# Cross-attention on one core: loads ordered by first use, attention values in one run, last projections in halves, new orders

## What is computed

```python
qh = _split_heads(q @ Wq.T + bq)          # q = x, 4 x 2048 x 512
kh = _split_heads(k @ Wk.T + bk)          # k = v = ctx, 4 x 77 x 512
vh = _split_heads(v @ Wv.T + bv)
scores = jnp.einsum('bhqd,bhkd->bhqk', qh, kh) / scale
scores = jnp.where(mask == 0, jnp.asarray(-1000000000.0, scores.dtype), scores)
m = jnp.max(scores, axis=-1, keepdims=True)
e = jnp.exp(scores - m) * mask.astype(scores.dtype)
probs = e / (jnp.sum(e, axis=-1, keepdims=True) + 1e-09)
attn = jnp.einsum('bhqk,bhkd->bhqd', probs, vh)
out = attn @ Wo.T + bo
x = out + residual
return (x - mu) / jnp.sqrt(var + 1e-05) * ln_g + ln_b
```

## Time and profile before

| | us |
|---|---|
| median of three runs | 617.84 (616.43 to 618.41) |
| the profiled execution | 615.88 |
| its span, first to last instruction | 614.1 |
| TensorE busy | 564.5 (92%) |
| VectorE busy | 525.6 (86%) |
| ScalarE busy | 504.6 (82%) |
| GpSimd busy | 437.5 (71%) |
| TensorE's mean granted clock | 0.985 |

### The profile page before, as it was taken

How to read it: one execution, slowest core, us unless ns; L and a number is a source line. 1 busy time by engine, 2 the same in 40 slices (tenths; PEclk the granted TensorE clock), 3 DMA queues, 4 the chain that set the end, 5 groups by cost and what they waited for, 6 DMA issues and landing times.

```text
span 614.1 us, 15264 instructions
## 1 busy us (share of the span) xinstructions
PE 564.5 (92%) x5460; PEld 456.9 (74%) x5460; DVE 525.6 (86%) x801; ACT 504.6 (82%) x2288; POOL 437.5 (71%) x399
## 2 busy tenths in 40 slices
PE   2699398999999999999999999999999999999795
PEld 2588376777878788777877788777878788776574
DVE  4577558789998979898998989898998899899877
ACT  4449669899898989998898989998898999889521
POOL 2704443867588795789778886689678967786787
PEclk9989789999999999999999999999999999999899
DMA  8922730120045310640324412340424312202132
GB/s 310 318 88 57 225 88 1 52 99 3 11 140 188 138 53 10 216 147 3 94 93 155 155 64 75 122 148 3 126 76 141 153 51 104 105 2 99 76 138 102
DMA packets 36198, 64.91 MB, mean 106 GB/s; under 512 B 12443, under 2 KB 14491, under 8 KB 34075
## 3 DMA queue, kind: packets, MB, share of 16 engines
q1 hardware_dynamic: 35979, 63.94, 30.6%
q10 hardware_dynamic: 144, 0.00, 0.0%
HBM read 44.15 MB, written 19.46 MB: 104 GB/s over the span
## 4 chain that ended last, share of the span: by engine, by line
PE 84%; DVE 6%; SPq 5%; DMA 3%; issue 2%; POOL 0%; ACT 0%; DVEq 0%
PE qo_bank L420 54%; PE s_bank L420 17%; PE av_bank L508 11%; DVE E L803 2%; DMA Kd<-TP 2%; PE av_bank L420 1%; DMA Vp<-V_scratch 1%; DVE TP L832 1%; SPq L251 1%; SPq L330 1%; SPq L256 1%; DVE qo_bank L849 1%; DVE bn L855 1%; SPq L304 0%; DVE AT_lo L841 0%
## 5 line engine op out<-in xcount | busy, mean ns | idle before, releaser
L625 ACT ACTIVATE E<-E,neg_max 128x77 f32<-128x77 f32 x1024 | 352.2, 352 | 19.7 <-DVE neg_max L811 19.6
L625 ACT ACTIVATION_READ_ACCUMULATOR E<-E,neg_max 128x1 f32 x1024 | 196.8, 192 | 0.0
L1125 POOL TENSOR_TENSOR E<-E,inv_sum 128x1232 f32<-128x1232 f32 x64 | 145.7, 2279 | 66.6 <-DVE inv_sum L818 66.6
L803 DVE TENSOR_TENSOR E<-s_bank,mask_bias 128x616 f32<-128x616 f32 x128 | 101.3, 791 | 40.7 <-PE s_bank L420 38.9
L420 PE MATMUL s_bank<-Kd,QT_hi 128*128 128x308 f32 x512 | 111.7, 305 | 0.0
L832 DVE STREAM_TRANSPOSE TP<-E 128x1280 f32<-128x1280 f32 x64 | 96.1, 1502 | 4.1 <-PE av_bank L508 3.6
L811 DVE TENSOR_REDUCE neg_max<-E 128x8 f32<-128x624 f32 x128 | 98.5, 781 | 0.4
L420 PE MATMUL s_bank<-Kd,QT_lo 128*128 128x308 f32 x256 | 81.3, 317 | 15.5 <-DVE E L803 11.7
L420 PEld LDWEIGHTS s_bank<-Kd,QT_hi 128*128 128x128 f32 x512 | 84.4, 188 | 4.2
L1143 POOL TENSOR_TENSOR Y<-Y,b_row 128x512 f32<-128x512 f32 x62 | 79.2, 1297 | 4.5 <-ACT Y L642 4.2
L1105 POOL TENSOR_TENSOR xT_lo<-xT_raw,xT_hi 128x1024 fp32r<-128x1024 f32 x30 | 71.7, 2410 | 14.0 <-ACT xT_hi L602 14.0
(11 more groups left out here) (60 smaller groups left out, 790.9 us busy)
## 6 DMA issues: line engine op xcount, KB each, us to landing
Y<-in_x SPq DMA_DIRECT2D x16, 1024.0 KB, 6.1
out_y<-Y SPq DMA_DIRECT2D x64, 256.0 KB, 2.0
xT_raw<-in_xT SPq DMA_DIRECT2D x15, 1024.0 KB, 4.9
Vp<-V_scratch SPq DMA_DIRECT2D x32, 96.0 KB, 2.4
K_scratch<-TP SPq DMA_DIRECT2D x1, 1232.0 KB, 6.8
Y<-in_WqT SPq DMA_DIRECT2D x4, 256.0 KB, 8.4
xT_raw<-in_xT SPq DMA_DIRECT2D x2, 512.0 KB, 6.9
TP<-in_WvT SPq DMA_DIRECT2D x4, 256.0 KB, 7.9
```

The source lines that it names most:

```text
L625: last = cp(e, e, ACT.Exp, bias=neg_max[:, t, h:h + 1], accum_out=rowsum[:, t, h:h + 1])
L803: tt(E[:, t, :, 0:SK].rearrange("p (g j) k -> p g j k", g=2), s_bank[:, :, 0:GK].rearrange("p g (j k) -> p g j k", j=HG), mask_bias[:, row ...
L1125: nc.gpsimd.tensor_tensor(out=e, in0=e, in1=inv.unsqueeze(2).broadcast_to((P, 2 * HH, SK)), op=ALU.mult).then_inc(probs_ready, 1)
```

## The change

The transfers of the opening are put in another order: x of block 0 goes ahead of `WqT`, in two pieces with a semaphore each (`x_first`), x of block 1 ahead of the mask, and `load_K(0)` is issued ahead of all later weights (`later_loads`), of which `WqT`'s second half now leads. Block 1's high part is made by GpSimd (`XT_hi_1`), its low part by VectorE (`XT_lo_first(1, i)`), and GpSimd also casts the second half of `WqT` (`split_hi_q`). On TensorE the two halves of `AV` stand next to each other in every block, where 13 of 16 blocks had a score unit between them. The output projection of block 14 is cut into two parts of six matmuls (`OUT_first` with channels 0 and 1, then `OUT` with channels 2 and 3), its last two row groups in `s_bank`. `S` itself, the tiles and all arithmetic stay. The orders of all five engines are new: `OUT` runs one turn later against the scores than it did, loads of x are issued in the turns before their use, and the written-out turns at both ends differ. Of the diff the parts that the text speaks of are shown; the new orders of ScalarE, VectorE and the rest of GpSimd's are left out, as are TensorE's turns 4, 14 and 15, of which 4 and 14 keep three neighbouring scores as the even pattern has them.

```diff
+        x_first = [sem(f"x_first{i}") for i in range(2)]
+        x1_hi = sem("x1_hi")
+        wq_hi_1 = sem("wq_hi_1")
...
+        QO_TURN = ((("Q", 1, 1), ("OUT", 4, 0), ("Q", 1, 2), ("OUT", 4, 1), ("Q", 1, 3),
+                    ("OUT", 4, 2), ("OUT", 4, 3), ("Q", 0, 0)),
+                   (("Q", 1, 1), ("OUT", 4, 0), ("Q", 1, 2), ("Q", 1, 3), ("OUT", 4, 1),
+                    ("OUT", 4, 2), ("OUT", 4, 3), ("Q", 0, 0)))
...
+        def split_out(o):
+            return o == NB - 2
+
+        def out_bank(o, k):
+            return s_bank[:, k - 2, :] if split_out(o) and k >= 2 else qo("OUT", o, k)[:, :]
...
-                for i in range(2 if b == 0 else 1):
-                    cs = slice(2 * i, 2 * i + 2) if b == 0 else slice(0, C)
-                    sp.dma_start(xT_raw[:, b % 2, cs, :], xT[b, :, cs, :]).then_inc(x_loaded[b % 2], 16)
+                sp.dma_start(xT_raw[:, b % 2, :, :], xT[b]).then_inc(x_loaded[b % 2], 16)
+
+            def load_xT_first():
+                for i in range(2):
+                    cs = slice(2 * i, 2 * i + 2)
+                    sp.dma_start(xT_raw[:, 0, cs, :], xT[0, :, cs, :]).then_inc(x_first[i], 16)
...
             load_half("k", WkT, 0)
+            load_xT_first()
             load_half("q", WqT, 0)
-            load_xT(0)
+            load_xT(1)
             sp.dma_start(mask_i, mask).then_inc(mask_loaded, 16)
-            load_xT(1)
-            load_half("k", WkT, 1)
-            load_half("q", WqT, 1)
-            for c in range(C):
-                load_w("v", WvT, c)
-            load_row(bv_loaded, bv_row[:, :], bv)
-            zero_V()
-            for c in range(C):
-                load_w("o", WoT, c)
-            load_row(bo_loaded, bo_row[:, :], bo)
-            load_row(rows_loaded, g_row[:, :], ln_g)
-            load_row(rows_loaded, b_row[:, :], ln_b)
+
+            def later_loads():
+                load_half("q", WqT, 1)
+                load_half("k", WkT, 1)
+                for c in range(C):
+                    load_w("v", WvT, c)
+                load_row(bv_loaded, bv_row[:, :], bv)
+                zero_V()
+                for c in range(C):
+                    load_w("o", WoT, c)
+                load_row(bo_loaded, bo_row[:, :], bo)
+                load_row(rows_loaded, g_row[:, :], ln_g)
+                load_row(rows_loaded, b_row[:, :], ln_b)
+
             for s in range(-3, NB + 6):
+                if s == -3:
+                    next_xT(0), next_xT(1), load_K(0), later_loads(), save_K()
+                elif s == -2:
+                    next_xT(2)
...
-                    next_xT(s - 2), next_xT(s - 1), next_K(s - 2), next_K(s - 1), store(s - 6, 0)
-                    store(s - 6, 1), store(s - 6, 2), store(s - 6, 3), store(s - 5, 0), load_rows(s - 4)
-                    store(s - 5, 1), store(s - 5, 2), store(s - 5, 3)
+                    next_K(s - 1), store(s - 5, 0), store(s - 5, 1), store(s - 5, 2), store(s - 5, 3)
+                    load_rows(s - 3), next_xT(s), next_xT(s + 1), next_V(s - 1)
                 else:
-                    load_rows(s - 5), store(s - 6, 0), store(s - 6, 1), store(s - 6, 2), store(s - 6, 3)
+                    store(s - 5, 0), store(s - 5, 1), store(s - 5, 2), store(s - 5, 3), next_V(s - 1)
+                    next_K(s - 1), load_rows(s - 3)
...
+            def OUT_part(o, k, cs, first, last):
+                pair, j = o // 2, 4 * (o % 2) + k
+                i, cols = j // 2, slice(j % 2 * P, j % 2 * P + P)
+                pe.wait_ge(at_lo, 4 * (2 * pair + cs[-1] // 2) + i + 1)
+                products = [(a[:, AT_PLACE[2 * pair + c // 2, i], c % 2, cols], w[:, c, :])
+                            for a, w in ((AT_hi, WoT_lo), (AT_lo, WoT_hi), (AT_hi, WoT_hi)) for c in cs]
+                for n, (a, b) in enumerate(products):
+                    done = mm(out_bank(o, k), a, b, start=first and n == 0, stop=last and n == len(products) - 1)
+                return done
+
+            def OUT_first(o, k):
+                if not has(o):
+                    return
+                if k < 2:
+                    qo_free("OUT", o, k)
+                else:
+                    pe.wait_ge(biased, T2 * NB)
+                OUT_part(o, k, (0, 1), True, False)
+
             def OUT(o, k):
                 if not has(o):
                     return
+                if split_out(o):
+                    OUT_part(o, k, (2, 3), False, True).then_inc(out_ps, 1)
+                    return
                 qo_free("OUT", o, k)
-                pair, j = o // 2, 4 * (o % 2) + k
-                i, cols = j // 2, slice(j % 2 * P, j % 2 * P + P)
-                pe.wait_ge(at_lo, 4 * (2 * pair + 1) + i + 1)
                 if o == 0 and k == 0:
                     pe.wait_ge(w_lo["o"], C)
-                accumulate(qo("OUT", o, k)[:, :],
-                           [(a[:, AT_PLACE[2 * pair + c // 2, i], c % 2, cols], w[:, c, :])
-                            for a, w in ((AT_hi, WoT_lo), (AT_lo, WoT_hi), (AT_hi, WoT_hi)) for c in range(C)]) \
-                    .then_inc(out_ps, 1)
+                OUT_part(o, k, range(C), True, True).then_inc(out_ps, 1)
 
             for s in range(-3, NB + 6):
                 if s == -3:
-                    K(0), K(1)
+                    K(0), K(1), Q(0, 0), Q(0, 1), Q(0, 2), S(0, 0), K(2), K(3), S(0, 1), Q(0, 3), S(0, 2)
+                elif s == -2:
+                    V(0), S(0, 3)
                 elif s == -1:
-                    Q(0, 0), Q(0, 1)
+                    V(1), V(2), S(0, 4), Q(1, 0), S(0, 5)
                 elif s == 0:
-                    K(2), K(3), S(0, 0)
+                    Q(1, 1)
                 elif s == 1:
-                    Q(0, 2), S(0, 1), Q(0, 3), S(0, 2), V(0), S(0, 3), V(1), S(0, 4), V(2), S(0, 5), Q(1, 0)
-                    S(0, 6), Q(1, 1), S(0, 7), Q(1, 2), S(1, 0), Q(1, 3), S(1, 1), S(1, 2), AV(0, 0)
-                    AV(0, 1), S(1, 3), S(1, 4)
+                    S(0, 6), S(0, 7)
                 elif s == 2:
-                    Q(2, 0), S(1, 5), Q(2, 1), S(1, 6), Q(2, 2), S(1, 7), S(2, 0), Q(2, 3), S(2, 1), S(2, 2)
-                    S(2, 3), Q(3, 0), S(2, 4), AV(1, 0), S(2, 5)
+                    Q(1, 2), Q(1, 3), S(1, 0), S(1, 1), S(1, 2), S(1, 3), Q(2, 0), S(1, 4), S(1, 5)
+                    AV(0, 0), AV(0, 1), S(1, 6)
                 elif s == 3:
-                    AV(1, 1), S(2, 6), Q(3, 1), OUT(0, 0), Q(3, 2), Q(3, 3), OUT(0, 1), S(2, 7), S(3, 0)
-                    OUT(0, 2), S(3, 1), OUT(0, 3), S(3, 2), Q(4, 0), S(3, 3), AV(2, 0)
-                elif s == 13:
-                    AV(11, 1), Q(13, 1), S(12, 5), OUT(10, 0), S(12, 6), Q(13, 2), OUT(10, 1), S(12, 7)
-                    Q(13, 3), S(13, 0), OUT(10, 2), S(13, 1), OUT(10, 3), S(13, 2), Q(14, 0), S(13, 3)
-                    AV(12, 0)
+                    Q(2, 1), S(1, 7), S(2, 0), Q(2, 2), Q(2, 3), S(2, 1), S(2, 2), S(2, 3), Q(3, 0)
+                    AV(1, 0), AV(1, 1), S(2, 4)
...
                 elif s == 16:
-                    S(15, 2), S(15, 3), AV(14, 0), S(15, 4), AV(14, 1), S(15, 5), OUT(13, 0)
+                    S(14, 2), Q(15, 0), S(14, 3), AV(13, 0), AV(13, 1), S(14, 4), Q(15, 1), S(14, 5)
+                    OUT(12, 0), S(14, 6), Q(15, 2), S(14, 7), OUT(12, 1), S(15, 0), Q(15, 3), S(15, 1)
+                    OUT(12, 2), OUT(12, 3)
                 elif s == 17:
-                    S(15, 6), S(15, 7), OUT(13, 1), OUT(13, 2), OUT(13, 3)
+                    S(15, 2), S(15, 3), S(15, 4)
                 elif s == 18:
-                    AV(15, 0), AV(15, 1)
+                    AV(14, 0), AV(14, 1), S(15, 5)
+                elif s == 19:
+                    pass
+                elif s == 20:
+                    OUT(13, 0), S(15, 6), S(15, 7)
                 elif s == 21:
-                    OUT(14, 0), OUT(14, 1), OUT(14, 2), OUT(14, 3), OUT(15, 0), OUT(15, 1), OUT(15, 2)
-                    OUT(15, 3)
+                    OUT(13, 1), OUT(13, 2), OUT(13, 3), OUT_first(14, 0), AV(15, 0), AV(15, 1)
+                    OUT_first(14, 1), OUT(14, 0), OUT(14, 1), OUT_first(14, 2), OUT_first(14, 3), OUT(14, 2)
+                    OUT(14, 3), OUT(15, 0), OUT(15, 1), OUT(15, 2), OUT(15, 3)
                 elif s % 2 == 0:
-                    S(s - 1, 4), AV(s - 2, 1), S(s - 1, 5), Q(s, 1), OUT(s - 3, 0), S(s - 1, 6), Q(s, 2)
-                    S(s - 1, 7), OUT(s - 3, 1), S(s, 0), Q(s, 3), OUT(s - 3, 2), S(s, 1), OUT(s - 3, 3)
-                    S(s, 2), Q(s + 1, 0), S(s, 3), AV(s - 1, 0), S(s, 4)
+                    AV(s - 3, 0), AV(s - 3, 1), S(s - 2, 4), Q(s - 1, 1), S(s - 2, 5), OUT(s - 4, 0)
+                    S(s - 2, 6), Q(s - 1, 2), OUT(s - 4, 1), S(s - 2, 7), Q(s - 1, 3), S(s - 1, 0)
+                    OUT(s - 4, 2), OUT(s - 4, 3), S(s - 1, 1), S(s - 1, 2), S(s - 1, 3), Q(s, 0)
+                    S(s - 1, 4), AV(s - 2, 0), AV(s - 2, 1), S(s - 1, 5)
                 else:
```

(37 more changed lines are left out.)

686 lines of the change are left out of this document (323 added, 363 removed).

## The result

The changed kernel took 623.22 us (621.5 to 626.03, four executions) against 617.13 for the kernel before: a ratio of 1.0106, interval 1.0054 to 1.0157. The forecast was 614.8, a gain of 3. The profiled execution took 621.89, with a span of 620.1; the sum had 611.1.

| stage | before | forecast | changed |
|---|---|---|---|
| start to end of `AV(2)` | 149.67 | 139.6 | 144.93 |
| to end of `AV(12)` | 342.35 | 347.7 | 351.83 |
| to the end | 122.1 | 123.8 | 123.3 |

A forecast was written before the change was run, and what follows sets the result against it. It took TensorE's own list to bound the middle, with waits counting at both ends. Opening -10.0, middle +5.3 and ending +1.7 gave -3.0, carried from the median 617.84 to 614.8 us, range 605 to 623.

The forecast's parts named there:

- Step (f): Opening: `Vp` load issued near 64, landing near 71; `turn(0, 3)` late next; `AV(0)` runs from 73.3 to 77.5.
- step (g): Opening: after `AV(1)`, TensorE's own units bring `AV(2)` to its end at 139.6 against 149.67, the -10.0.
- Steps (a) to (d): Opening: first matmul at 8.2 instead of 11.28, no wait at `Q(0, 0)`, 0.7 allowed at `Q(0, 2)`, `S(0, 0)` at 22.5.
- (c): Opening: `Q(0, 2)` needs x of block 1, cast and subtracted near 19, when TensorE arrives; 0.7 allowed.
- Step (e): Opening: `K(2)` waits about 3 for `WkT`'s late second half, and what follows is slow; 4.5 counted.
- (i): Middle: an `S` directly follows an `S` in 10 places instead of 4; six more at 1.18 are +7.1.
- (h): Middle: `AV` in one run saves 0.34 a block, 3.4 over the ten blocks from `AV(3)` to `AV(12)`.
- (j): Middle: whole `AV` runs may break off, costing 0 to 0.8 a block; two of ten taken, 1.6.
- (k): Middle: VectorE keeps up, 32.9 a block against 34.6, three margins under 0.5; 0 taken, 1 us per block as bad end.
- Rival (2): Every `AV` in one run breaks off: 13 more runs at 0.8, 10.4 instead of 1.6; 623.6, slower; chance 0.12.
- Rival (4): Opening gives half: `WkT` split meets GpSimd's casts, exponentials start 4 us later; -6 instead of -10, 618.8; chance 0.12.
- Rivals (1) and (3): (1): waits cheaper, no `AV` breaks, ending gains, 607.5, chance 0.22. (3): VectorE bounds the middle, 620.8, chance 0.12.

The follow-up runs named there:

- the second profile: The changed kernel timed and profiled again with no edit, beside the kernel before: 625.94 us, ratio 1.0140.
- keys_early: The changed kernel with `load_K(1)` issued ahead of `next_xT(2)` on SyncE: 618.68 us, ratio 1.0038 to the kernel before.
- merged_halves: Changed kernel's opening with early keys' load, then the kernel before's order, `AV` halves apart, `S(s - 1, 7)` ahead of `Q(s, 3)`, `center` moved earlier: 604.09 us, ratio 0.9788.
- join_center_first: As before_join, with `center(s - 4, 3)` ahead of `bias(s - 1, 4)` on VectorE in the even turns 4 to 14: 619.60 us, ratio 1.0044.
- one_pair: The changed kernel with the three scores in a row taken apart in even turns, five direct S-S successions instead of ten: 617.21 us, ratio 1.0011.
- far_pairs: As one_pair, plus a second S-S succession in the odd turns: ten successions, none right behind another: 625.80 us, ratio 1.0158.
- before_join: The kernel before with the two halves of `AV` joined for blocks 2 to 12: 635.32 us, ratio 1.0295.
- before_nopair: As before_join, with `S(s - 1, 7)` ahead of `Q(s, 3)` in odd turns 5 to 11, so no direct S-S succession: 634.12 us, ratio 1.0274.
- merged: The changed kernel's opening with `load_K(1)` ahead of `next_xT(2)`, then the order of before_nopair with the kernel before's ending: 626.16 us, ratio 1.0149.
- halves: The changed kernel with the two halves of `AV` apart again in turns 5 to 14, one S between them: ratio 1.0143 to the kernel before.

## Why the prediction missed, step by step
**The opening, -10.0 forecast, -4.7 measured in the first profile and -0.4 in the second.** Step (f) failed. It lists `load_K(1)` behind `next_xT(2)` in SyncE's queue and prices only what the order does to `Vp`, which was issued at 61.20 and cost nothing. The queue has a second customer: `turn(0, 0)`, because `TP` is at once the place of the raw keys. With that one load moved, `AV(0)` started at 72.20, for which the prediction had 73.3; with it as changed, at 78.15 and, in the second profile, 79.42. That is 5 to 6 us of the miss, in the first profile nearly all of it. From the start of `AV(0)` to the end of `AV(2)` step (g) counted 66.3 and the first profile took 66.8; the second and keys_early took 69.9 and 70.0, each with two falls of 3.4 us in this stretch, for which (g) has no term.

Steps (a) to (d) held but for one wait: first matmul at 7.75 (8.2), `S(0, 0)` at 22.90 (22.5), and (c) had no wait (0.7 allowed); `Q(0, 0)` waited 1.0 for the split of `WqT`, where (b) had none. Step (e) was too dear: `K(2)` and the unit behind it stood for 0.42 and 1.09, at full clock behind it, where 4.5 were counted. The first exponential came at 37.01 (38.5).

By the rule of the Trainium skill that the prediction cites ("SBUF — State Buffer", "SBUF: two separate sides") each of the two `XT_lo_first(1, i)` could have lost the length of a cast. The view of that line (count; shortest, median and longest in ns; first and last start in us):

```profile
L823 DVE TENSOR_TENSOR xT_lo<-xT_raw,xT_hi x2: 1211/1618/2025, 15.9 to 17.8; 128x1024 fp32r<-128x1024 f32 x2
```

Only the first met a cast: it started at 15.9, GpSimd's second cast (1.04 long) ended at 16.8, and it took 2.03, against 1.23 for block 0's. The second met none and took 1.21. So where the two met, the loss of 0.80 is near the rule's; the prediction had counted on two meetings. Both were done at 19.05, before TensorE came to `Q(0, 2)` at 20.09. The row that the prediction takes for the price of a meeting, 2246 ns, is a mean of 1.6 and 2.9 us, so that one meeting there cost up to 2.2, not 1.6.

**The middle, +5.3 forecast, +9.5 measured.** (i) held: a row of three scores at full clock takes 0.87 + 2 x 2.01 = 4.89; five rows are 11.4 more than fifteen single scores, and the four pairs of before were 4.7 more, so +6.7 for the +7.1 of the sum. (h) held: ten runs without their breaks are 3.6 shorter than twenty halves with entries and restarts (3.4). (j) had the right sum with some luck: it counted two breaks of 0.8, and there were three, which made their runs 0.3, 0.8 and 0.6 longer, 1.6 in all by the unrounded rows (1.9 in the second profile). The Trainium skill's sentence that fetching is mostly hidden ("Runtime: NRT & Kernel Launch", "Instruction fetch mechanics") would have made them 0; the measurement decides, and that fetching is what breaks the runs is not shown. What the sum has no term for is the clock: three falls at 1.5 are 4.5. -3.6 + 6.7 + 1.6 + 4.5 = 9.2 of the 9.5. The prediction treated each wait as a thing by itself with the price 1.18; in a row of two the price was 1.14 each and, in three places of five, 1.5 on top. (k) held, no wait of that kind came.

**The ending, +1.7 forecast, +1.3 measured.** `AV(15)` started 90.2 after the end of `AV(12)` (89.0), the last matmul ended at 116.0 (115.8), `OUT(13, 3)` waited 2.96 (3.5). One step is off without a trace in the sum: the last exponential ended 82.7 after `AV(12)`, not 78.6.

**The carry to the median** had no part in the miss: 621.89 against a median of 623.22, and 615.88 against 617.13.

**The rivals.** Rival (2), a break in every run, has the number nearest to the measured one (623.6), but not its cause: only every third run broke, for 1.6 in the middle. Rival (4) had the size of the opening (-6), but by weights and a late first exponential, and neither happened. Rivals (1) and (3) did not come.

**What is shown and what is argued.** Shown by an edit of its own: the keys' load (keys_early), that the middle of the kernel before improves by 3.7 without its four pairs and is then TensorE alone (merged_halves), and the queue behind `bias` (join_center_first). Read from the clock's record: three falls in the middle, 1.5 us each. Supported by one profiled execution of each kernel, and not more: that waits in a row and not the number of waits go with the falls (one_pair and far_pairs against the changed kernel). Open: why a fall comes in some places and executions and not in others.

## What to carry to other kernels
When a transfer is moved back in a queue, list everyone who waits for it, including those who want the place it reads from; the consumer of the data is only one of them. Put waits of the busiest engine apart: here two waits with little work between cost more than twice one in three places of five. When a unit moves on one engine, look at what stands behind its partner on the next engine, and put ahead of it what was ready before.

## What the hardware showed that I had not expected
**The clock falls behind short waits.** Behind rows with two waits of 0.9 between the marks it fell in 9 of 15 places (the changed kernel twice, keys_early), always the same three of five; behind rows with three in 3 of 5; behind `AV`, `S` and a wait of 1.55 or more in 12 of 15 (before_join, before_nopair, merged). Behind single waits for `bias` of up to 1.5 us between the marks in none of 25 places (the kernel before, one_pair, far_pairs, join_center_first). Most falls last about 3.4 us and cost 1.5. Each profile is one execution. The two openings of the changed kernel and the mean clocks of the executions without a profile show that a fall can come in one execution and not in the next. In the opening, single waits of 3.7 and 2.2 were followed by falls as well, the second not in every profile.

**Runs of 192 matmuls break off in every third block.** In every kernel with whole runs they are those of blocks 4, 7, 10 and 13 (and 1, where it is a run), some 15 to 24 matmuls before the end, for up to 0.9 us, with no engine to wait for; the other blocks never, and halves never. In some profiles a single one of these breaks is too short to be seen (block 4 of one_pair, under 0.1). A run with a break is longer by up to 1.4. From the timeline of join_center_first, the rest of block 7's run:

```profile
317.95 0.67 PE L478 MATMUL av_bank<-TP,Vp 32*32 32x256 f32 x16 [0.40 <-issue]
```

A fixed place in the stream of instructions is a likely part of the cause: it is 16 matmuls before the end in block 7 and 15 in block 13 in every kernel, and in block 4 24 in the changed kernel's order and 17 in that of before. It isn't enough by itself, since the halves of the same blocks ran through (halves). No run here tried to move it.
